# One attention kernel on one core: Keys' piece two steps later, waits left out, one copy in fourteen by VectorE

## What is computed

```python
x = x + tanh(g_xattn) * xattn(layernorm(x), ctx, ctx, 0, mask)
x = x + tanh(g_ffn) * ffn(layernorm(x), ...)

# xattn, for each of 8 batches, 8 groups of 4 heads that share keys and values of 64 numbers:
scores = einsum("bsgrd,btgd->bgrst", q, k) / sqrt(64) + mask     # 224 rows x 750 context rows
out = einsum("bgrst,btgd->bsgrd", softmax(scores), v)
```

## Time and profile before

| | |
|---|---|
| median of 3 runs | 1101.99 us (1100.58 to 1102.91) |
| the profiled execution | 1101.88 us |
| its span in the profile | 1100.0 us |
| busy: TensorE, ScalarE, VectorE, GpSimd | 1054.5, 873.7, 861.8, 827.4 us |
| attention | from the start to about 816 us |

### The profile page before, as it was taken

The page is one execution under the profiler, slowest core; times in us unless marked ns, Lnnn a source line. Parts: engine busy times, 40 slices in busy tenths (PEclk is TensorE's granted clock), DMA queues, the critical chain, the costliest instruction groups (busy, mean ns, idle before and its releaser), DMA issues.

```text
span 1100.0 us, 42843 instructions
## 1 busy us (share of the span) xinstructions
PE 1054.5 (96%) x18241; PEld 764.5 (69%) x18276; DVE 861.8 (78%) x2134; ACT 873.7 (79%) x1159; POOL 827.4 (75%) x600
## 2 busy tenths in 40 slices
PE   4999999999999999999999999999979999999998
PEld 2777777777777777777777777777757555555554
DVE  4877887888788888878887888888754998767776
ACT  3999999999999999999999999999932435655545
POOL 4999999999999999999999999999840212414324
PEclk9999999999999999999999999999999999999999
DMA  8244544443443434434344443243148100011224
GB/s 246 73 132 145 151 104 136 132 123 93 117 117 97 104 107 121 103 106 122 97 104 108 126 108 82 74 108 102 47 152 290 61 1 1 1 78 77 115 101 168
DMA packets 131872, 119.02 MB, mean 108 GB/s; under 512 B 90338, under 2 KB 114786, under 8 KB 127843
## 3 DMA queue, kind: packets, MB, share of 16 engines
q1 hardware_dynamic: 130962, 115.24, 36.3%
q10 hardware_dynamic: 720, 1.05, 0.3%
HBM read 83.47 MB, written 20.97 MB: 95 GB/s over the span
## 4 chain that ended last, share of the span: by engine, by line
PE 65%; POOL 14%; ACT 10%; issue 8%; DVE 2%; DMA 1%; POOLq 0%; DVEq 0%; ACTq 0%
PE psum L1007 13%; PE psum L1063 13%; PE psum L993 12%; POOL arena L636 10%; PE psum L1039 6%; ACT arena L799 5%; PE psum L1027 5%; PE psum L1028 5%; ACT arena L803 4%; PE psum L1149 3%; PE psum L1050 2%; PE psum L967 2%; PE psum L1118 1%; POOL arena L601 1%; PE psum L1188 1%
## 5 line engine op out<-in xcount | busy, mean ns | idle before, releaser
L636 POOL TENSOR_TENSOR arena<-arena 128x1536 bf16<-128x1536 f32 x224 | 614.4, 2748 | 26.4 <-ACT arena L799 25.8
L1419 DVE CUSTOM_DVE_ANT_0 arena<-psum,arena 128x750 f32<-128x750 f32 x448 | 405.3, 937 | 108.7 <-PE psum L993 95.0
L803 ACT ACTIVATE arena<-arena,neg_max 128x750 f32<-128x750 f32 x448 | 411.7, 919 | 4.4 <-DVE neg_max L1419 4.4
L799 ACT ACTIVATE arena<-psum 128x768 f32<-128x768 f32 x448 | 361.3, 807 | 49.3 <-PE psum L1007 23.6
L1007 PE MATMUL psum<-ident,arena 64*128 64x64 f32 x5376 | 264.1, 232 | 18.8 <-ACT arena L799 17.9
L1007 PEld LDWEIGHTS psum<-ident,arena 64*128 64x128 f32 x5376 | 202.7, 139 | 87.0 <-ACT arena L799 67.3
L993 PE MATMUL psum<-arena 64*128 64x512 bf16 (+1 forms) x2688 | 259.6, 325 | 3.7 <-DVE neg_max L1419 2.2
L1027 PE MATMUL psum<-arena 128*128 128x65 bf16 (+1 forms) x2688 | 199.0, 195 | 0.0
L1028 PE MATMUL psum<-arena 128*128 128x64 bf16 (+1 forms) x2688 | 198.5, 194 | 0.0
L993 PEld LDWEIGHTS psum<-arena 64*128 64x128 bf16 x2688 | 122.9, 95 | 92.5 <-issue 4.5
L1027 PEld LDWEIGHTS psum<-arena 128*128 128x128 bf16 (+1 forms) x2688 | 177.6, 98 | 0.1
(11 more groups left out here) (168 smaller groups left out, 1084.9 us busy)
## 6 DMA issues: line engine op xcount, KB each, us to landing
arena<-in_k_t SPq DMA_DIRECT2D x128, 187.5 KB, 3.3
arena<-in_v_rows SPq DMA_DIRECT2D x64, 192.0 KB, 3.6
arena<-in_k_t SPq DMA_DIRECT2D x122, 93.8 KB, 2.7
arena<-arena SPq DMA_DIRECT2D x244, 46.9 KB, 2.4
out<-arena SPq DMA_DIRECT2D x10, 1024.0 KB, 3.9
arena<-in_x_top SPq DMA_DIRECT2D x8, 1024.0 KB, 6.1
arena<-in_x_rest SPq DMA_DIRECT2D x8, 768.0 KB, 5.7
spill<-arena SPq DMA_DIRECT2D x96, 64.0 KB, 2.2
```

The source lines that it names most:

```text
L636: pool.tensor_tensor(p_lo[:, slots, :], p_sb[:, slots, :], high(p_sb[:, slots, :]), ALU.subtract).then_inc(p_split, 1)
L799: act.activation(p_sb[:, n % RING, :].rearrange("p (c h q) -> p h c q", h=2, q=HALF), turned_ps, ACT.Copy).then_inc(evac_a, 1)
L803: act.activation(s_sb[:, n % RING, 0:CTX], s_sb[:, n % RING, 0:CTX], ACT.Exp, bias=neg_max[:, n % 4, :], scale=-1.0).then_inc(exped, 1)
L1419: dve.tensor_tensor_reduce(s_sb[:, n % RING, 0:CTX], flat_ps[:, score_at(s):score_at(s) + CTX], mask_sb[:, max(m - REP + 1, 0), :], -1.0, ...
```

## The change

Four things. GpSimd's piece for the keys of the group after the next one goes from p = 4 to p = 6, W1's piece from p = 6 to p = 4, and the first roots of the second part from p = 5 to p = 3. Of each pass's units the tenth (`DVE_COPY = 5`: the first of step 5) is copied from PSUM to `p_sb` by VectorE, at the head of its round p = 4, before the maxima; it counts on a semaphore of its own, `evac_v`, and whoever waited for `evac_a` now waits by `wait_copies` for the one or the other. The turn of unit 11 waits in addition for its exponentials, which the order of ScalarE's list told it before. And TensorE leaves out waits: for the queries' low halves in the steps after the first that uses them, and for the copies ahead of `value_high`, which the turns before it have waited for.

```diff
+        evac_v = sem("evac_v")
...
+        DVE_COPY = 5
+
+        def copied_by_dve(n):
+            return n % (2 * UNITS) == 2 * DVE_COPY
+
+        def dve_copies(n):
+            return (n + 2 * UNITS - 2 * DVE_COPY - 1) // (2 * UNITS)
+
+        def wait_copies(eng, n):
+            last = n - 1
+            if copied_by_dve(last):
+                eng.wait_ge(evac_v, dve_copies(n))
+            else:
+                eng.wait_ge(evac_a, n - dve_copies(n))
...
@@ GpSimd @@
-                    pool.wait_ge(evac_a, 2 * j + 2)
+                    if copied_by_dve(2 * j):
+                        wait_copies(pool, 2 * j + 1)
+                    wait_copies(pool, 2 * j + 2)
...
                     if p == 2:
                         split_k(2 * both + 3)
-                    if p == 4 and both + 2 < PAIRS:
-                        split_k(2 * both + 4)
                     if p == 5:
                         split_v(2 * both + 2)
+                    if p == 6 and both + 2 < PAIRS:
+                        split_k(2 * both + 4)
...
-                if p == 6 and 3 <= both < 3 + KC:
+                if p == 4 and 3 <= both < 3 + KC:
                     n = both - 3
...
-                if both == PAIRS - 1 and p == 5:
+                if both == PAIRS - 1 and p == 3:
                     root2(0, EARLY)
@@ ScalarE @@
-                    if 0 <= i + 1 < NP:
+                    if 0 <= i + 1 < NP and not copied_by_dve(2 * (i + 1) + s):
                         copy_unit(2 * (i + 1) + s)
@@ TensorE: score_pair, turn_unit, value_high, sum_query @@
-                if both == 0:
-                    pe.wait_ge(q_split, 1 if p < 2 else 2 if p < 4 else 3)
-                else:
-                    pe.wait_ge(q_split, parts_split(both, 0 if p < 4 else 1))
+                if both == 0 and p in (0, 2, 4):
+                    pe.wait_ge(q_split, 1 + p // 2)
+                elif both > 0 and p in (0, 4):
+                    pe.wait_ge(q_split, parts_split(both, p // 4))
...
-                    pe.wait_ge(evac_a, n)
+                    if copied_by_dve(n - 1):
+                        pe.wait_ge(exped, n + 1)
+                    wait_copies(pe, n)
...
-                    pe.wait_ge(evac_a, n + 1)
+                    if j == NP - 1:
+                        wait_copies(pe, n + 1)
...
-                    pe.wait_ge(evac_a, NU)
+                    wait_copies(pe, NU)
@@ VectorE @@
             for i in range(FIRST, NP + 1):
                 both, p = place(i)
+                n = 2 * (i + 1)
+                if 0 <= n < NU and copied_by_dve(n):
+                    dve.wait_ge(turned, n + 1)
+                    dve.wait_ge(p_split, n // 2 - 1)
+                    dve.tensor_copy(p_sb[:, n % RING, :].rearrange("p (c h q) -> p h c q", h=2, q=HALF), turned_ps).then_inc(evac_v, 1)
```

## The result

The changed kernel takes 1117.41 us (median of 4 runs, 1116.79 to 1117.87) against 1102.32 of the kernel before beside it: a ratio of 1.0139, interval 1.0122 to 1.0157. It is 15.1 us slower; 11.7 was forecast, and the time lies in the range of 1108 to 1119. In the changed kernel line 1030 is the turn, 820 ScalarE's copy, 657 the low halves, 1438 VectorE's copy, 1014 the scores, 1448 the maxima, 1296 and 1309 the statistics and their merge, 614 keys' piece, 1074 the turn of staged rows (1399).

The account below looks back on a forecast made before the run. The prediction took the copy of each step's first unit, on TensorE's path, as the bound, with GpSimd second. It summed 1101.9 + 18.7 (late copies) - 6.7 (GpSimd) - 0.3 (tail) = 1113.6 us, range 1108 to 1119.

Parts of the forecast that it names:

- the late copies at step 5: Step 5 of the passes: VectorE's copies start late behind statistics and take longer, 18.7 us lost in sum.
- What bounds the kernel: Attention steps: the copy of a step's first unit is on TensorE's path, the second's has cover; GpSimd is second.
- The copy's start: Round 4: behind two statistics and merge late by 0.98, behind two statistics by 0.69; with length, 1.13 and 0.84.
- The copy's length and what the turn adds: Step 5: VectorE's copy takes 0.96 against ScalarE's 0.81, so 0.15 longer, bounds 0 and 0.25; unit 11's added wait 0.
- rival 2: VectorE's copy runs at two elements a cycle, about 0.56 long, costing 9.7: 1104.6 us; chance 0.04.
- GpSimd's pieces: Rounds 4 to 6: exchanging keys' and W1's pieces removes ScalarE's waits for GpSimd, 6.7 us gained, ends 4 and 8.9.
- Waits left out: TensorE's queue: these waits are over before TensorE comes to them, so leaving them out gains 0.
- The tail: End of attention: a new wait for VectorE's last copy replaces that for staged rows; 0.3 gained, ends -2.0 and +1.7.
- 1: Late copies are absorbed in waits TensorE has anyway in later steps, only 7.0 of gains stay: 1094.9 us; chance 0.11.
- 3: ScalarE's relief carries on to the normalisations, up to 0.8 in each of seven passes, 5.6: 1108.0 us; chance 0.06.
- 4: GpSimd's gain doesn't come, as its pieces still follow each other and waits only move: 1120.3 us; chance 0.07.
- 5: The new tail wait adds to the old, with its own low-clock stretch, + 4.2: 1117.8 us; chance 0.06.

Follow-up runs that it names:

- old rounds: The changed kernel with keys' piece back in p = 4 and W1's in p = 6: 1116.02 us, ratio 1.0139 to the kernel before.
- statistics behind: The changed kernel with round 3's statistics and merge moved to round 4, after VectorE's copy: 1106.67 us, ratio 1.003 to the kernel before.
- order of waits: The changed kernel with the two waits ahead of unit 11's turn swapped, the copy's first, the exponentials' second: 1113.66 us in a single run.
- the copy at its best: The changed kernel with statistics after the copy, the copy's wait put first and the last pass copied by ScalarE: 1102.73 us, ratio 1.0015 to the kernel before.
- pieces alone: The kernel before with only keys' and W1's GpSimd pieces exchanged between rounds 4 and 6: 1096.60 us, ratio 0.9939.
- waits alone: The kernel before with only the waits for low halves and for copies ahead of the high halves' products left out: 1101.05 us, ratio 0.9995.

## Why the prediction was right, and where it was off

The total came out for the forecast's main reason, the late copies at step 5. Two of its terms were not what it said, and that the second of them, GpSimd's, did no harm to the sum is luck.

*What bounds the kernel.* Right. The turn of a step's second unit follows the copy of the first, and each delay of that copy comes through whole: 20.1 at step 5. The steps of units 5 and 7 in the passes with normalisations kept their 3.71 and 4.89, as forecast.

*The copy's start.* Right, and nearly exact: 1.11 measured for 1.13, 0.86 for 0.84. Moving the statistics behind the copy made all passes equal, so this is shown and not only argued. Pass 8, counted at nothing, cost 0.17.

*The copy's length and what the turn adds.* The copy takes 0.94 in the median, near the 0.96 interpolated, so rival 2 with its 0.56 falls. But a quiet pass cost 0.24 and not 0.15. The missing 0.09 is the second semaphore ahead of the turn; the forecast named it, bounded it and then took it at 0, and the swapped waits give 0.09 back. With statistics ahead it hardly shows, since two small errors met it: in pass 9 the copy was 0.94 late and not 0.98, and with 0.89 only 0.08 longer than ScalarE's; 0.09 on top makes the 1.11.

*GpSimd's pieces.* The size was right (6.7, and 6.7 in the other steps), the reason was not enough. The forecast added this gain to the copies' loss as if they were apart. Alone the exchange gives 6.3; beside the late copy it gives nothing, because the loss already contains the same slack (the run with the old rounds). The sum came out because it held that gain once, which was luck: a forecast of the exchange's worth in this kernel, against the copy alone, would have said 7 and met nothing.

*Waits left out.* 0, and 0 measured.

*The tail.* Its path was right and its size wrong: 0.3 was to be gained, and 2.0 were lost. TensorE, first at the wait and then behind it, in the changed kernel:

```profile
809.74 0.59 PE L1030 MATMUL psum<-ident,arena 64*128 64x64 f32 x12
...
815.44 0.90 PE L1030 MATMUL psum<-ident,arena 64*128 64x64 f32 x12 [5.11 <-DVE arena L1438]
...
820.17 0.90 PE L1030 MATMUL psum<-ident,arena 64*128 64x64 f32 x12 [0.90 <-ACT arena L820]
...
822.97 1.94 PE L1074 MATMUL psum<-ident,arena 128*128 128x128 f32 x8
```

VectorE beside it, and the stretches behind (columns as in rows 2):

```profile
813.43 1.00 DVE L1399 TENSOR_SCALAR arena<-arena,mv_all,rstd_all 128x512 f32<-128x512 f32 x2 [3.54 <-POOL rstd_all L633]
814.35 0.95 DVE L1438 COPY arena<-psum 128x768 f32<-128x768 f32 x1
```

```profile
816.00:820.00 4.00, 3.27 (x55) 2.87 (x52) 1.88 (x9) 2.32 (x3) 2.67 (x1) 0.50 0.87 332
820.00:824.00 4.00, 3.83 (x53) 3.71 (x54) 0.00 (x0) 0.93 (x2) 2.07 (x2) 0.50 0.00 1
```

The chain is the forecast one: root, both stagings, copy, turn; and the staged rows are no longer waited for. The second turn comes 5.70 after the first where it came 1.50 after it before (796.47 and 797.97), so it is 4.2 later, as forecast; the idle time of 5.11 is that and the 0.91 which stood before this turn already. What the forecast took at nothing is the clock. From 814.52, still in this wait, to 824.76 the granted clock is 0.50, the lower of the two levels (1.2 GHz), for 10.2 us, where it was so for 3.4 before: the turns take 0.90 instead of 0.59 and the staged rows' 1.94 instead of 1.07. Two other kernels with the same tail show what the path is worth by itself. Where the low stretch lasts 3.4 as before (statistics behind, order of waits), the tail takes 27.2 and 27.1, 0.5 and 0.6 less than the 27.7 before, where the forecast said 0.3. And of the executions with statistics behind, the three with a mean granted clock of 0.998 took 1105.4 to 1105.7, and six of the seven with 0.995 took 1107.3 to 1107.5, 1.8 more (the seventh 1105.9). All four executions of the changed kernel show 0.995. So the clock turns the gain into the loss; the forecast had +1.7 as an end and not in its sum. Against the run with the last copy by ScalarE (no such stretch, but a locked staging) the whole is 4.1.

*The sum.* Forecast +18.7 - 6.7 - 0.3 = 11.7; measured on the profiles' spans +20.1 - 6.7 + 2.0 = 15.4. The rivals: 1 fell in what it said of the copies, though a part of it was true of GpSimd's lateness, which they absorbed; 3 fell with the copy at its best. Of 4, GpSimd's waits did go; but that the exchange gives nothing here, as 4 had it, is so for another reason. Of 5, the low clock came, and the old wait did not.

## What to carry to other kernels

An engine's share of busy time says little on whether it wants relief: ScalarE was at 94% and gave up 22 us of work for nothing, while two normalisations in every fourth pass, taken from the place where it really was late, gave 7. Before an engine takes over a piece of the critical path, read what stands ahead of that piece in its queue, in each kind of pass, and what then stands behind. And two changes that both give slack to the same late engine don't add: cost them together, and run each alone.

## What the runs showed of the hardware that was not expected

- The order of two semaphore waits ahead of one instruction matters: 0.09 us a time when the one that ends last stands second, measured over 12 equal passes (3.51 against 3.42), in one execution of each kernel.
- Staging of 2 x 512 f32 numbers took 1.00 us on VectorE alone and 5.85 beside GpSimd's low halves, in each of seven kernels with that tail; cut into 5 and 3 heads, the same operation on as many numbers in the middle of the kernel ran beside them without a lock, at 1.06 for both parts instead of 0.54.
- The low clock at the end of the attention differs between profiles of the same tail. With the old tail it lasted 3.4, 6.8 and 6.8 us (before, pieces alone, waits alone); with the changed one 10.2, 6.8, 3.4 and 3.4 (changed, old rounds, statistics behind, order of waits); in the seven kernels with the last copy by ScalarE there was none three times and 3.4 four times. What decides it stays open. All four executions of the changed kernel show the mean clock of its profile, 0.995.
- Not tried: the tail's staging split like the normalisations. By its 5.85 against 1.00 and TensorE's wait of 2.23 it would be the next place to look.
